# Layer two's queries and keys computed with features on partitions, read back in 2 KB pieces, in a kernel of two transformer layers

## The reference

```python
xn = _layernorm(x)
x = x + _L0_attn_ref(xn, ...) + _L0_ffn_ref(xn, w_gating, w_linear)     # causal, 32 heads of 8; fp8 gelu feed-forward
xn = _layernorm(x)
x = x + _L1_attn_ref(xn, ...) + _L1_ffn_ref(xn, w_gate_up, w_proj)
```

```python
q = (x @ wq.T).reshape(b, s, 16, 16);  k, v likewise
def apply_rope(x, inv_freq):              # sin, cos of position * inv_freq, 8 frequencies
    x1, x2 = (x[..., ::2], x[..., 1::2])
    return jnp.concatenate([x1 * cos - x2 * sin, x1 * sin + x2 * cos], axis=-1)
scores = jnp.einsum('bshd,bstd->bsht', q, k) / 4
attn = jnp.einsum('bsht,bstd->bshd', softmax(scores), v)
```

## Time and profile before

| | us |
|---|---|
| median of 3 runs | 562.63 |
| lowest, highest | 561.89, 563.28 |
| the profiled execution | 563.48 |
| its span in the trace | 561.7 |
| TensorE busy | 532.6 |
| ScalarE busy | 468.4 |
| VectorE busy | 389.4 |
| GpSimd busy | 235.5 |

### The profile page before, as it was taken

How to read it: one execution, slowest core, us unless ns; L and a number is a source line. 1 busy time by engine, 2 the same in 40 slices (tenths; PEclk the granted TensorE clock), 3 DMA queues, 4 the chain that set the end, 5 groups by cost and what they waited for, 6 DMA issues and landing times.

```text
span 561.7 us, 12578 instructions
## 1 busy us (share of the span) xinstructions
PE 532.6 (95%) x4767; PEld 260.9 (46%) x4767; DVE 389.4 (69%) x845; ACT 468.4 (83%) x607; POOL 235.5 (42%) x302
## 2 busy tenths in 40 slices
PE   7779788999999999999999999999999999998995
PEld 3323244333444555545545454564445353456663
DVE  5766798977868678767788975749445435568673
ACT  2399999999999999999899889879899888873541
POOL 2677856443452357152765764143253120260100
PEclk9989999999999999999999999999999999999998
DMA  8923210311343516241323626554444154157954
GB/s 268 289 62 100 57 24 10 85 30 38 49 85 53 104 34 96 62 78 24 82 28 67 125 50 82 82 81 89 88 86 70 33 105 67 32 102 123 135 110 97
DMA packets 214398, 46.08 MB, mean 82 GB/s; under 512 B 197440, under 2 KB 213056, under 8 KB 214336
## 3 DMA queue, kind: packets, MB, share of 16 engines
q1 hardware_dynamic: 213760, 44.93, 41.0%
q10 hardware_dynamic: 576, 0.33, 0.4%
HBM read 19.02 MB, written 10.49 MB: 53 GB/s over the span
## 4 chain that ended last, share of the span: by engine, by line
PE 73%; DMA 8%; DVE 5%; ACT 4%; SPq 3%; issue 3%; POOL 2%; DVEq 0%; POOLq 0%; ACTq 0%
PE psV L713 21%; PE psS L699 8%; PE psA L882 3%; PE psC L789 3%; PE psB L882 3%; PE psC L882 3%; PE psS L835 2%; ACT Pt L965 2%; PE psB L892 2%; PE psA L892 2%; DMA at<-oscr 2%; PE psB L846 2%; PE psA L750 2%; PE psA L789 2%; PE psC L750 1%
## 5 line engine op out<-in xcount | busy, mean ns | idle before, releaser
L965 ACT ACTIVATE Pt<-psS 128x1024 f32<-128x1024 f32 x288 | 280.1, 1031 | 24.0 <-PE psS L699 20.0
L713 PE MATMUL psV<-Pt,vaug 128*32 128x512 f32 x1152 | 149.0, 602 | 1.5 <-POOL Pt L1640 1.4
L1640 POOL TENSOR_SCALAR_AFFINE_SELECT Pt<-Pt 128x1024 f32<-128x1024 f32 x64 | 71.8, 1147 | 77.1 <-ACT Pt L965 76.9
L699 PE MATMUL psS<-qTf,kTf 32*128 32x512 f16 x576 | 64.7, 386 | 5.6 <-ACT Pt L965 3.1
L699 PEld LDWEIGHTS psS<-qTf,kTf 32*128 32x128 f16 x576 | 17.7, 91 | 84.0 <-ACT Pt L965 50.0
L1690 POOL TENSOR_TENSOR ss<-ss,mhalf 128x1 f32<-128x1 f32 x16 | 9.6, 598 | 85.7 <-DVE ss L1477 85.7
L713 PEld LDWEIGHTS psV<-Pt,vaug 128*32 128x32 f32 x1152 | 25.4, 108 | 42.7 <-issue 34.7
L1023 ACT ACTIVATE stage<-psS 128x1024 f32<-128x1024 f32 x32 | 31.1, 1024 | 7.0 <-PE psS L835 6.9
L1631 POOL TENSOR_TENSOR QXf<-rt,QXf 128x512 f16<-128x512 f32 x16 | 19.8, 1240 | 26.6 <-ACT QXf L952 26.6
L1311 DVE SCALAR_TENSOR_TENSOR gw<-gw,gb 128x512 f32<-128x512 f32 x32 | 27.7, 866 | 4.8 <-ACT gw L980 4.8
L882 PE MATMUL psA<-wguT,xhs 128*128 128x512 bf16 x108 | 27.8, 380 | 0.0
(11 more groups left out here) (355 smaller groups left out, 1136.2 us busy)
## 6 DMA issues: line engine op xcount, KB each, us to landing
qkvscr<-rqkv SPq DMA_DIRECT2D x16, 384.0 KB, 2.7
G<-qkvscr SPq DMA_DIRECT2D x24, 128.0 KB, 3.9
stage<-in_wg SPq DMA_DIRECT2D x4, 512.0 KB, 8.4
w8g<-qkvscr SPq DMA_DIRECT2D x16, 128.0 KB, 3.7
oscr<-o SPq DMA_DIRECT2D x16, 128.0 KB, 3.2
at<-oscr SPq DMA_DIRECT2D x16, 128.0 KB, 2.5
out<-yout SPq DMA_DIRECT2D x16, 128.0 KB, 2.3
x<-in_x SPq DMA_DIRECT2D x1, 1536.0 KB, 12.5
```

The costliest lines, as they stand in the source:

```text
L699: e.matmul(psS[j], kd[32 * j:32 * j + k, h, 128 * at:128 * at + 128], qd[32 * j:32 * j + k, 4 * h:4 * h + 4, :].rearrange("p s n -> p (s n ...
L713: ins = e.matmul(psV[32 * j:32 * j + 32, :], vaug[:, at, j, 32 * h:32 * h + 32], Pt[(4 * Q + j) % NP], start=(kb == 0 and h == 0), stop=(k ...
L965: e.activation(flat(Pt4[:, u % NP:u % NP + 2, :]), flat(psS4[:, j:j + 2, :]), ACT.Exp, scale=scale).then_inc(S["exp"], 1)
L1640: e.affine_select(out=p, in_=p, pattern=[[0, 8], [1, 128]], compare_op=ALU.is_ge, fill=0.0, base=0, channel_multiplier=-1).then_inc(S["mas ...
```

## The change

For a tile of layer two's first pass:

- `qkv1` part 0 has weights and input exchanged: 24 matmuls of 128 columns give queries and keys with features on partitions, in four blocks of 128 columns (even and odd features, q and k). The columns of the weights are sorted for that on the host (`turn`).
- The turn by position then needs tables with features on partitions: `sin` computes two more of 1024 columns, `tT` transposes them (16 transposes in four steps), `tTc` copies them, once.
- `rab` (VectorE) multiplies straight out of PSUM, two operations of 512 columns; `rr` (GpSimd) subtracts and adds, 256 columns each. `qk1c`, `ro1`, `ro1p`, `ro2` leave the first pass.
- `rw` writes the two halves to memory in 128-byte pieces, `rd` reads them back in four transfers of 16 partitions with 2 KB pieces into qk1T, feature by feature. `mk` puts the indicator rows there, once. `kq` (ScalarE) copies both, queries and keys, from qk1T to consecutive columns in kTf. `gT`, `gTq` and `gTk` leave the first pass. The tile qk1T is single: `rd` waits for `kq` of the tile before.
- A group is 16 heads by eight positions as before, but now eight positions 16 apart, so that the values are written in 64-byte pieces and read in 1 KB pieces (`vw`, `vr`); the result is written in 1 KB pieces and read in 64-byte pieces (`ow`, `at1r`).
- The loads at the start become steps and are sorted anew: two of the fp8 weight pieces come on ScalarE's queue (`wgx`), x from tile 4 on in three later pieces there (`lx`), the raw weights of layer two after the fourth `w8` (`lw`).
- Several buffers share one array `big`; `ORDER` and the counts of `warm` (62 matmuls to 39) are new.

```diff
-WARM = (10, 16, 8, 10, 12, 3, 3)
+KQ = 2
+WARM = (9, 3, 2, 7, 5, 11, 2)
...
-    "xn1T": lambda n: ("xn1f", n - NT + 1), "qkv1": lambda m: ("v1c" if m % 2 else "qk1c", m // 2 + 1),
+    "xn1T": lambda n: ("xn1f", n - NT + 1), "qkv1": lambda m: ("v1c", m // 2 + 1) if m % 2 else ("rab", m + 2) if m < 2 * NT else ("qk1c", m // 2 - NT + 1),
+        qk1 = [big[:, 3072:3584]]
-        qk1Todd = flat(kTf[:])[:, 1280:2304].rearrange("p (s j n) -> p s j n", s=2, n=128)
+        qk1Tg = flat(kTf[:])[:, 1280:2304].rearrange("p (s j n) -> p s j n", s=2, n=128)
...
+        def landed(s):
+            return qk1T[:, s, :, :].rearrange("p j n -> p (j n)").rearrange("p (h j a) -> p j h a", j=4, a=8)
+
+        def of_group(n, s, b, j):
+
+            if n >= NT:
+                return turned(n, s)[32 * b:32 * b + 25, j, :]
+            return turned(n, s)[32 * b:32 * b + 24, j, :]
+
...
+            def lw(n):
+                w.wait_ge("w8", 4)
...
-                w.wait_ge("w8", min(k - 1, 6))
+                w.wait_ge("w8", 0 if k < 2 else min(k - 3, 6))
...
             def vw(n):
                 w.wait_ge("v1c", n + 1)
-                w.wait_ge("ro2", 2 * n + 2)
-                w.wait_ge("d_vr", 48 * (n - NT + 1))
-                e.dma_start(qkvscr[n % NT].rearrange("s p c -> p s c"), rqkv[n % 2][:]).then_inc(S[f"d_vw{n % 2}"], 16)
+                if n < NT:
+                    e.dma_start(vscr[n].rearrange("h t d -> t h d"),
+                                rqkv[n % 2][:, 2, :].rearrange("p (h d) -> p h d", d=16)).then_inc(S[f"d_vw{n % 2}"], 16)
...
             def vr(n):
                 w.wait_ge(f"d_vw{n % 2}", 16 * (n // 2 + 1))
                 w.wait_ge("PV1", n - 1 if n < NT else n)
-                w.wait_ge("gz", 4 if odd(n) else 2)
-                src = qkvscr[n % NT].rearrange("s (g a) (b d) -> (a b) s g d", a=8, d=16)
-                for s in range(3):
-                    e.dma_start(group(n, s)[:, :, 0:16], src[:, s, :, :]).then_inc(S["d_vr"], 16)
+                w.wait_ge("gz", 2)
+                if n < NT:
+                    e.dma_start(group(n, 2)[:, :, 0:16], vscr[n].rearrange("h (a g) d -> (h a) g d", g=16)).then_inc(
+                        S[f"d_vr{n % 2}"], 16)
...
+            def mk(k):
+                w.wait_ge("tc", 12)
+                for s in range(2):
+                    dst = qk1T[:, s, :, :].rearrange("p j n -> p (j n)")
+                    for b in range(4):
+                        e.dma_start(dst[32 * b + 16:32 * b + 24, :], A["ind2"][s]).then_inc(S["d_rd0"], 16)
+
+            def rw(n):
+                src = flat(rqkv[n % 2][:, 0:2, :]).rearrange("p (f m t) -> p f m t", f=2, t=32)
+                dst = rscr[n].rearrange("s b (f i) (h t) -> f (i h) (s b) t", f=2, t=32)
+                for f in range(2):
+                    w.wait_ge("rr", 2 * n + f + 1)
+                    e.dma_start(dst[f], src[:, f, :, :]).then_inc(S[f"d_rw{n % 2}"], 16)
+
+            def rd(n):
+                w.wait_ge(f"d_rw{n % 2}", 32 * (n // 2 + 1))
+                w.wait_ge("d_rd0", 128)
+                w.wait_ge("kq", KQ * n)
+                for b in range(4):
+                    dst = qk1T[32 * b:32 * b + 16, :, :, :].rearrange("p s j n -> p s (j n)")
+                    e.dma_start(dst, rscr[n, :, b].rearrange("s d n -> d s n")).then_inc(S[f"d_rd{n % 2}"], 16)
 
             def ow(n):
                 w.wait_ge("o1", 2 * n + 2)
                 w.wait_ge("d_or", 16 * (n - NT + 1))
-                e.dma_start(oscr[n % NT].rearrange("(g a) (b d) -> (a b) g d", a=8, d=16),
-                            o1_b[n % len(o1_b)][:]).then_inc(S["d_ow"], 16)
+                t = n % NT
+                dst = (o2scr[t].rearrange("h (a g) d -> (h a) g d", g=16) if n < NT else
+                       oscr[t].rearrange("(g a) (b d) -> (a b) g d", a=8, d=16))
+                e.dma_start(dst, o1_b[n % len(o1_b)][:]).then_inc(S["d_ow"], 16)
 
             def at1r(n):
                 w.wait_ge("d_ow", 16 * (n + 1))
                 w.wait_ge("at1T", n + 1 - len(at1))
-                e.dma_start(at1[n % len(at1)][:], oscr[n % NT]).then_inc(S["d_or"], 16)
+                if n < NT:
+                    e.dma_start(at1[n % len(at1)][:].rearrange("p (h d) -> p h d", d=16),
+                                o2scr[n].rearrange("h t d -> t h d")).then_inc(S["d_or"], 16)
...
+                    if part == 0:
+                        for c in range(4):
+                            for k, (pt, q, a) in enumerate(((0, 0, 0), (1, 0, 0), (0, 1, 0), (0, 0, 1), (1, 0, 1), (0, 1, 1))):
+                                ins = e.matmul(bank[:, 128 * c:128 * c + 128], wparts[:, q, a, 128 * c:128 * c + 128],
+                                               src[:, pt, 128 * a:128 * a + 128], start=(k == 0), stop=(k == 5))
+                        ins.then_inc(S["qkv1"], 1)
+                        return
...
+            def tT(m):
+                w.wait_ge("sin", 1)
+                w.wait_ge("d_id", 16)
+                bank = shared("tT", m)
+                for k in range(4):
+                    c0 = 512 * (m % 2) + 128 * k
+                    ins = e.transpose(bank[:, 128 * k:128 * k + 128], turns[:, 1 + m // 2, c0:c0 + 128], identf[:])
+                ins.then_inc(S["tT"], 1)
+
             def S1(n):
...
-                k = 24 if n < NT else 25
-                w.wait_ge("gTq", n + 1)
-                w.wait_ge("gTk", n + 1)
+                if n < NT:
+                    w.wait_ge("kq", KQ * (n + 1))
+                w.wait_ge("gTq", n - NT + 1)
+                w.wait_ge("gTk", n - NT + 1)
                 w.wait_ge("gTm", n - NT + 1)
                 for j in range(4):
                     for b in range(4):
                         scores_free("S1", n, b)
-                        ins = e.matmul(psS[b][:, 128 * j:128 * j + 128], turned(n, 1)[32 * b:32 * b + k, j, :],
-                                       turned(n, 0)[32 * b:32 * b + k, j, :], start=True, stop=True)
+                        ins = e.matmul(psS[b][:, 128 * j:128 * j + 128], of_group(n, 1, b, j), of_group(n, 0, b, j),
+                                       start=True, stop=True)
...
-                                       P1[:, 4 * j + c, :], start=True, stop=True)
+                                       P1[:, 4 * c + j if n < NT else 4 * j + c, :], start=True, stop=True)
...
+            def wgx(k):
+                e.dma_start(stmp[:, k % 2, :], A["wg"][k % 2, 128 * (k // 2):128 * (k // 2) + 128, :]).then_inc(
+                    S["d_wgd" if k % 2 else "d_wgc"], 16)
+
+            def lx(n):
+                xt = A["x"].rearrange("(t p) c -> p t c", p=128)
+                e.dma_start(x[:, 4 * n:4 * n + 4, :], xt[:, 4 * n:4 * n + 4, :]).then_inc(S["d_xa" if n == 1 else "d_xb"], 16)
...
+                e.activation(turns[:, 2, :].rearrange("p (m h) -> p m h", h=16),
+                             ang[:, 0, :].unsqueeze(2).to_broadcast([128, 64, 16]), ACT.Sin)
+                e.activation(turns[:, 1, :].rearrange("p (m h) -> p m h", h=16),
+                             ang[:, 2, :].unsqueeze(2).to_broadcast([128, 64, 16]), ACT.Sin, bias=hpi[:],
                              scale=-1.0).then_inc(S["sin"], 1)
...
+            def tTc(m):
+                if m == 4:
+                    w.wait_ge("tT", 4)
+                    w.wait_ge("tTc", 2)
+                    e.activation(turns[:, 2, :], turns[:, 0, :], ACT.Copy).then_inc(S["tTc"], 1)
+                    return
+                bank = psM[filled["tT", m] % len(psM)]
+                w.wait_ge("tT", m + 1)
+                e.activation(turns[:, m // 2, 512 * (m % 2):512 * (m % 2) + 512], bank[:], ACT.Copy,
+                             scale=1.0 / WUP).then_inc(S["tTc"], 1)
...
+            def kq(n):
+                w.wait_ge(f"d_rd{n % 2}", read_groups(n))
+                w.wait_ge("S1", 4 * n)
+                for s in range(2):
+                    e.activation(qk1Tg[:, s, :, :].rearrange("p j (h a) -> p j h a", a=8), landed(s), ACT.Copy).then_inc(S["kq"], 1)
...
+            def rab(n):
+                bank = psM[filled["qkv1", 2 * n] % len(psM)][:].rearrange("p (e s a c) -> p e s a c", e=2, s=2, a=8)
+                t0 = 128 * (n % NB)
+                w.wait_ge("tTc", 5)
+                w.wait_ge("tc", 12)
+                w.wait_ge("qkv1", 2 * n + 1)
+                w.wait_ge("rr", 2 * n)
+                for k in range(2):
+                    table = turns[:, k:k + 2, t0:t0 + 128].rearrange("p e (a c) -> p e a c", a=8)
+                    e.tensor_tensor(r1[:, k, :].rearrange("p (e s c a) -> p e s a c", e=2, s=2, a=8), bank,
+                                    table.unsqueeze(2).to_broadcast([128, 2, 2, 8, 16]), ALU.mult).then_inc(S["rab"], 1)
...
+            def rr(n):
+                dst = flat(rqkv[n % 2][:, 0:2, :])
+                w.wait_ge("rab", 2 * n + 2)
+                w.wait_ge(f"d_rw{n % 2}", 32 * (n // 2))
```

(6 more changed lines are left out.)

219 lines of the change are left out of this document (115 added, 104 removed), and 238 rows, old and new, of the table ORDER.

## The result

The changed kernel takes 559.68 us (median of 7 runs, 557.54 to 560.64) against 562.63 us: a ratio of 0.994, 95% interval 0.9917 to 0.9963. That is -2.95 us. The forecast was 557.2 us, -5.5, with a range of 548.5 to 565: right in direction, and about twice too large. The profiled execution took 560.62 us, its span is 558.9. The two profiled spans lie 2.8 us apart, as the medians do, so they may be compared.

What follows compares the result with a forecast made beforehand. TensorE and ScalarE were taken to bound it together before 240 us, TensorE from 240 to 498, neither after. Terms 0 + 3.5 - 5 - 4 = -5.5 us gave 557.2 us in the median's terms, range 548.5 to 565.

Steps and rivals of the forecast that it cites:

- Start: Up to the first exponential: stays at 29.7 us, where its table load ends; 0, bounds -1.5 and +2.5 us.
- First exponential to quad 64: ScalarE's net additions of about +6 us partly vanish in its 7.8 us of idle: +3.5 us, bounds 0 and +6.
- Quads 64 to 143: 240 to 498 us, TensorE full: removed transposes less the changed step give -7, of which -5 us comes out.
- VectorE (nothing): Multiplies out of PSUM priced as a 0.69 us copy; some -20 us of work on an engine busy 69%, counted as nothing.
- kq (0.65 each): Two new ScalarE copies a tile, 128 x 512 from SBUF, priced at 0.65 us each like L991.
- Tail: From quad 143 to the end: last down projection begins some 4 us sooner; -4 us, bounds -8 and +1.
- The walk: Tail estimate stepping the new order through traced durations: queries-to-scores route 11.7 us if SyncE is free, 21.9 before.
- ScalarE keeps up: Rival: its additions vanish in idle time, TensorE's -7 comes out whole, tail gives 7; about 548 us, chance 0.20.
- ScalarE binds everywhere: Rival: exponentials set the pace to quad 143, +7, TensorE's -7 buys nothing, tail 0; 569 us, chance 0.09.
- Weight loads that show: Rival: the narrow matmuls' loads do not hide; about 572 us at 98 ns, 567 at 81 ns; chance 0.09.
- The transposes were not free in the middle: Answers a rival that the removed transposes had cost nothing, needing holes beside them; counted only within the case of cancelling.
- the case in which it cancels: Rival: the terms become +6, -3 and -3, within 0.3% of no change; 561 to 564 us, chance 0.12.

Runs made afterwards that it cites:

- ktearly: Changed kernel with the transposing transfers of tile 0's queries and keys ahead of a weight load on SyncE: 555.76 us, ratio 0.9874 to the kernel before.
- notab: Changed kernel without making the sine and cosine tables with features on partitions; a GpSimd fill gives a constant instead: 558.88 us, ratio 0.9939 to the kernel before.
- pad18: Changed kernel with 18 matmuls of 128 columns added before each queries-and-keys step (42 instead of 24): 572.28 us, ratio 1.0177 to the kernel before.
- gthalf: Kernel before, each of 32 steps of four transposes replaced by one bf16 matmul of 512 columns: 562.66 us, ratio 1.0009 to the kernel before.
- kq2: Changed kernel with each of the two ScalarE copies of queries and keys per tile made twice: 569.75 us, ratio 1.0123 to the kernel before.
- tail: Changed kernel, end reordered: result read and tile 15's four reads ahead of the hidden state's transfer, TensorE and VectorE steps moved: 565.44 us, ratio 1.0058 to before.
- tail2: Changed kernel with tile 15's four reads ahead of tile 11's output, and VectorE's last attention copy ahead of reductions: 557.56 us, ratio 0.9919 to the kernel before.
- read1k: Changed kernel reading the attention's result in 1 KB instead of 64-byte pieces, mixing heads and positions: 556.29 us, ratio 0.9887 to the kernel before.
- wide512: Changed kernel with the queries-and-keys step back to six matmuls of 512 columns, positions as weights: 557.21 us, ratio 0.9901 to the kernel before.

## Why the prediction was right, and where not

**Start (0; measured +0.8).** Wrong in its cause. I let the first exponential wait for its table load; that load had gone, and the keys of tile 0 came last, behind a weight load in SyncE's queue. ktearly showed it. The bounds of -1.5 and +2.5 held for this profile; kernels with the same transfers lie between -0.1 and +3.2.

**First exponential to quad 64 (+3.5; +1.2).** The term was too large, and it was made of the wrong parts. Quad 2 lost 2.4 us, 1.9 of them with ScalarE busy all the way with the sines and the table loads moved there; the other 0.5 come and go among kernels with this start. The copies of the tables cost some 2 us later on (notab). So ScalarE's additions cost about what I took, and from quad 2 to quad 64 the changed kernel is still 1.3 us faster than the one before. What gives back that much, the eight transposes of this stretch (3.9 us), VectorE's relief or the new order, no run separates. I had counted the transposes only as something that hides a part.

**Quads 64 to 143 (-5; -5.3).** Right in size, and mostly borne out in its cause. The transposes cost more than I had taken (0.51 us a step, not 0.465), TensorE's time is paid in full when added (pad18) and at 0.6 when taken away with nothing else changed (gthalf); so some 4.7 of the 5.3 us are theirs, if that price holds for all of it. I had taken 5 of 7, 0.7. The step of 24 matmuls takes 1.35 or 1.44 us by what follows it, where the old one takes 1.31 or 1.39: +0.04 us, forecast +0.03. That the old one's two times are those with and without a wait, as I had read them, is wrong: neither has a wait.

**VectorE (nothing).** Its price was wrong: each multiply out of PSUM takes 1.11 us in the mean of all 32, not 0.69 (one of three groups by shape, after), and VectorE lost 7.9 us of work, not some 20. It had the room.

```profile
L1512 DVE TENSOR_TENSOR r<-psC,big 128x512 f32<-128x512 f32 x14 | 14.5, 1120 | 8.9 <-PE psC L853 8.9
```

**kq (0.65 each).** 0.64 measured, right; but "it can follow", said of ScalarE, was too kind: kq2's copies are paid at 0.76 there.

**Tail (-4; +0.6).** The step that failed. The +0.6 is one profile, with the longest tail of five alike; the medians leave +1.2 us for start and tail together, so the 4 us are missing all the same. The walk took the route of queries and keys as 11.7 us "if SyncE is free" and took the result's read at its old price. SyncE was not free: the four reads stood behind the 64-byte read and an output, and S1 came after 21.7 us. But of tail and tail2, which issue these reads 6.2 and 3.7 us sooner (counted from quad 143), one lost and the other gained nothing that shows, so this route is not shown to be what held the end. And I had booked the swap of pieces between the result's write and read as even: it is the read that TensorE waits for, and read1k, with the old pieces, is 3 us faster, though wide512 leaves open how much of that is the pieces'. gthalf, which saved TensorE's time in the old tail too, shows the same from the other side: no gain at the end. One part of the walk held: gate step 60 does stand ahead of the wait now (528.65 us). That the hidden state's loop behind it, one buffer and a transfer a tile, had no slack is what tail shows.

**The sum (-5.5; -2.95).** That it comes within 2.5 us is partly luck: the stretch to quad 64 was taken 2.3 us too high, start and tail together some 5 us too low, and the errors have opposite signs.

**The rivals.** None of them came out as it was put. ScalarE keeps up and ScalarE binds everywhere are both refused by pad18 and kq2: work added to either engine is paid. Weight loads that show are refused by the step's 1.44 us. The transposes were not free in the middle (gthalf, 1.8 us), though the whole of gthalf did not move. The 559.68 us lie in the range of my forecast's own case, nearer to the case in which it cancels than to its centre.

## What to carry to other kernels

Where two engines form one chain, the price of a microsecond has to be measured where it is spent: added work was paid at 0.7 to 1.0 here, transposes taken from the old order bought 0.6 in the middle and nothing at the end, and 0.4 us taken from the new step bought 0.5. An experiment that leaves work out and puts a stand-in elsewhere (notab's fill) measures both: cut its profile where the work had stood. A steady middle hands on a shift of its start without loss (3.5 us here), so look first at what the first step of the steady part waits for, and whether its transfer stands behind one that waits for something else. In a tail of transfers, ask which of a write and its read back is waited for before you swap their pieces.

## What the runs showed of the hardware

- After a wait of 2.96, 3.85 or 4.20 us TensorE ran at the lower level for some of the next steps: a projection of 2.98 instead of 1.91 us, scores of 2.09 instead of 1.17, projections of 1.65 and 1.49 instead of 0.88 and 0.81. Behind a wait of 1.53 us (read1k) it kept the higher one, 1.91; behind one of 1.45 us in gthalf, with others before it, it was down at the scores 3 us later; and in ktearly the projections took 1.51 and 1.49 us behind a wait of 1.22 with shorter ones after it. The length of the last wait alone does not decide: in notab a wait of 2.97 us was followed by a projection of 1.91. In the changed kernel the 2.96 us of waiting cost another 1.1 in the projection behind it.
- A read of 128 KB in 64-byte pieces lands after 3.3 us in the median, in 1 KB pieces after 2.5, and the issue right behind it took 1.6 us in the median of nine (0.96 to 3.94, 2.88 in the tail shown), behind the long pieces 1.2 (0.38 to 3.75, 1.13 there).
- A multiply of 128 x 512 out of PSUM whose result is written at steps of eight elements takes 1.11 us on VectorE; a plain copy of that size 0.69. Whether the step or the second operand costs it, no run separates.
- 79 quads repeat to 0.1 us in nine profiles (247.2 us), and a delay at the start is there at their end unchanged. Of the one that arises between quads 2 and 6 in notab (2.9 us), 2.1 are gone by quad 34, and at least 1.0 of them between quads 19 and 20, where the table copies no longer stand.
